# Attention and a routed feed-forward: another order of TensorE's work, other PSUM banks, and another way of filling the key windows

## The reference, cut to what matters

```
x: 2 x 2048 x 256 f32; 16 heads of 16; local causal attention, 64 back
qkv    = x @ W_attn + b_attn
scores = q k^T / 4, masked to j <= i and j >= i - 64;  attn = softmax(scores)
x = layernorm(x + (attn v) @ W_proj + b_proj)
e      = argmax(x @ Wr^T)                       # one of 8 experts for each token
inter  = gelu(x @ W1[e] + b1[e])                # 256 -> 1024
x = layernorm(x + layernorm(inter @ Wo + bo + x) * gamma + beta)
```

## Time and profile before

| what | us |
|---|---|
| median of three runs | 518.16 |
| the profiled execution: time | 519.47 |
| its span | 517.7 |
| PE busy | 486.7 (94%) |
| DVE busy | 406.8 (79%) |
| ACT busy | 356.0 (69%) |
| POOL busy | 277.0 (54%) |

### The profile page before, as it was taken

One profiled execution on the slowest core, in us unless ns is written; L12 is line 12 of the kernel. 1 busy time (PEld: TensorE's weight loads), 2 busy tenths in 40 slices (PEclk: granted clock), 3 DMA queues, 4 the chain that ended last, 5 costly groups with the idle time before them and its releaser, 6 DMA issues. The chain is left out here.

```text
span 517.7 us, 24448 instructions
## 1 busy us (share of the span) xinstructions
PE 486.7 (94%) x8597; PEld 431.7 (83%) x8597; DVE 406.8 (79%) x1096; ACT 356.0 (69%) x796; POOL 277.0 (54%) x483
## 2 busy tenths in 40 slices
PE   7999999999999999999988899999999999999970
PEld 6778888888887888888876788899999999999960
DVE  5658888778877897789789748988888877887771
ACT  6676868686867786777767566666666667666850
POOL 8712546454555455544543347666667566556553
PEclk9999999999999999999999899999999999999995
DMA  7785767786776696768662122222355555522100
GB/s 206 224 237 160 210 205 204 199 237 204 224 208 202 190 268 177 213 198 242 184 176 81 52 79 68 74 76 73 86 173 177 168 173 197 194 75 70 41 23 8
DMA packets 90183, 80.96 MB, mean 156 GB/s; under 512 B 36502, under 2 KB 83871, under 8 KB 90018
## 3 DMA queue, kind: packets, MB, share of 16 engines
q1 hardware_dynamic: 86720, 70.95, 47.6%
q0 software_dynamic: 3248, 8.41, 4.4%
q10 hardware_dynamic: 98, 0.04, 0.0%
HBM read 43.50 MB, written 23.55 MB: 130 GB/s over the span
## 5 line engine op out<-in xcount | busy, mean ns | idle before, releaser
L1423 PE MATMUL ps<-v_even,w_hi 128*128 128x128 f16 x1024 | 139.3, 219 | 0.5 <-issue 0.4
L1405 PE MATMUL ps<-wo_hi,ks 128*128 128x256 f16 (+1 forms) x576 | 128.5, 273 | 2.5 <-DVE ks L1099 2.5
L839 ACT ACTIVATE probs<-ps,b1T 128x128 f32<-128x128 f32 (+1 forms) x312 | 85.5, 360 | 59.5 <-PE ps L1423 37.5
L1423 PE MATMUL ps<-v_even,w_lo 128*128 128x128 f16 x512 | 107.9, 219 | 0.0
L1423 PEld LDWEIGHTS ps<-v_even,w_hi 128*128 x1024 | 96.4, 98 | 2.5 <-issue 1.0
L1166 DVE TENSOR_REDUCE mx<-ps 128x4 bf16<-128x512 f32 x128 | 82.9, 684 | 8.4 <-PE ps L1474 8.2
L1405 PE MATMUL ps<-wo_lo,ks 128*128 128x256 f16 (+1 forms) x288 | 78.5, 273 | 0.0
L1523 PE MATMUL ps<-v_even,probs 128*64 128x17 f32 x1024 | 70.2, 210 | 1.8 <-issue 1.8
L858 ACT ACTIVATE probs<-ps 128x512 f32<-128x512 f32 x128 | 69.6, 611 | 2.5 <-PE ps L1500 1.6
L1523 PE MATMUL ps<-v_odd,probs 128*64 128x17 f32 x1024 | 70.1, 210 | 0.6 <-issue 0.6
L1523 PEld LDWEIGHTS ps<-v_even,probs 128*64 128x64 f32 x1024 | 65.2, 138 | 5.7 <-issue 5.0
(11 more groups left out here) (245 smaller groups left out, 1237.7 us busy)
## 6 DMA issues: line engine op xcount, KB each, us to landing
qk_s<-qk_room SPq DMA_DIRECT2D x32, 256.0 KB, 2.8
w_in<-in_L_ffn_W_dram SPq DMA_DIRECT2D x16, 512.0 KB, 5.6
v_odd<-slots SPq DMA_DIRECT2D x64, 128.0 KB
qs<-qk_s SPq DMA_DIRECT2D x16, 384.0 KB
ks<-qk_s SPq DMA_DIRECT2D x16, 384.0 KB, 5.2
ks<-qk_s SPq DMA_DIRECT2D x32, 144.0 KB
v_even<-v_odd SPq DMA_DIRECT2D x63, 68.0 KB, 3.2
qk_s<-qk_room SPq DMA_DIRECT2D x32, 128.0 KB, 3.1
```

The lines of the kernel that those rows point to most:

```text
L839: last = nc.scalar.activation(g[1 - p][:, ic, n * w:(n + 1) * w], ps_h[1 - p][:, half, col + n * w:col + (n + 1) * w], ACT.Gelu, bias=b1T[ ...
L1405: ins = mm(ps_y[p][0:m], h[p][hs][:, ic, 0:m], wo[ws][:, ic, :], start=n == 0, stop=n == 3 * IC - 1)
L1423: up_ins = mm(ps_h[1 - p][:, half, col + m * w:col + (m + 1) * w], weights(ws, m, k, ic), sT[1 - p][ss][:, k, at], start=k + n == 0, stop= ...
```

## The change

PE's order in a turn becomes: projection, transposes of x, scores 0 and 1, values 0, scores 2 and 3, values 1, next values, transposes of the maxima (now a full 128 columns), queries and keys, transposes of the attention, transposed scores with the ranks between. The projection moves to bank 6, the transposes of x to bank 4, the ranks to bank 2 (the last of each stay in bank 1), so that several waits go and others come. DVE takes `y` and the logits first in its turn, ahead of the maxima; the splits of `w1` go in pairs into even turns, one ahead of DVE's copy of the transposed attention and one behind it. ACT copies the values of tile `it` at the head of turn `it`, behind the last exponentials of the tile before, where it copied those of `it + 1` in the middle of the turn before. SP stores each pair's queries and keys in two DMAs with nothing written twice, loads queries and block 1 in three DMAs each at the head of an even turn, and fills the window from block 1 by two SBUF to SBUF copies in the odd turn. The first pair keeps the old way.

```diff
-    qk_s = nc.dram_tensor("qk_s", [2, TILES // 2, P, 3, CC, 2 * P], f16, kind="Internal").ap()
+    qk_0 = nc.dram_tensor("qk_0", [2, P, 3, CC, 2 * P], f16, kind="Internal").ap()
+    qk_s = nc.dram_tensor("qk_s", [2, TILES // 2, P, 2, CC, 2 * P], f16, kind="Internal").ap()
...
-        mx = [sb(f"mx{k}", [P, P - ALIGNED], bf16) for k in range(2)]
+        mx = [sb(f"mx{k}", [P, P], bf16) for k in range(2)]
...
-            return ps[:, 0 if t >= LEAD else 4 + t % 2, 0:CC * P].rearrange("p (k t) -> p k t", k=CC)
+            return ps[:, 4 if t >= LEAD else 4 + t % 2, 0:CC * P].rearrange("p (k t) -> p k t", k=CC)
...
-        ps_proj = ps[:, 1, 0:C + E]
+        def ps_proj(t):
+            return ps[:, 6 if t < TILES - 1 else 1, 0:C + E]
...
+        def w1_lows(it):
+
+            lows_at = range(it - 2, it if it % 2 == 0 else it - 2) if it < TILES - 3 else w1_halves(it)
+            return [n for n in lows_at if a_tile(n)]
...
+            def stack(g, w, dst, landing):
+
+                for j in range(3):
+                    rows = dst[2 * j:ALIGNED:6]
+                    sp.dma_start(rows.rearrange("r (h m) n -> r h (m n)", m=CC),
+                                 qk_s[PARTS[w][j], g].rearrange("(h d) w m n -> w d h (m n)", d=HD)[w]).then_inc(landing, 16)
 
             def stacks_begin(g):
...
-                windows(g, 0, new, stack_ld[k])
+                stack(g, 0, qs[k], stack_ld[k])
+                if g > 1:
+                    sp.wait_ge(window_ld[1 - k], 16 * window_loads(g - 1))
+                stack(g, 1, ks[k][:, 1, :, :], second_ld[k])
 
             def stacks_end(g):
...
+                sp.wait_ge(second_ld[k], 16 * second_loads(g))
+                sp.dma_start(ks[k][0:ALIGNED:2, 0, :, BLK:2 * P], ks[k][0:ALIGNED:2, 1, :, 0:2 * P - BLK]).then_inc(window_ld[k], 16)
+                sp.wait_ge(second_ld[1 - k], 16 * second_loads(g - 1))
+                sp.dma_start(ks[k][0:ALIGNED:2, 0, :, 0:BLK], ks[1 - k][0:ALIGNED:2, 1, :, 2 * P - BLK:2 * P]).then_inc(window_ld[k], 16)
...
+                        if g > 0:
+                            sp.dma_start(qk_s[part, g].rearrange("p w m n -> p (w m n)"),
+                                         qk[g % 2][part].rearrange("p w m n -> p (w m n)")).then_inc(qk_st[g % 2], 16)
...
+                if a_tile(it - 1) and it < LAST - 2:
+                    exps(3, it - 1)
+                if a_tile(it) and it > 0:
+                    copy_v(it)
...
                 if cur:
+                    exps(0)
                     exps(1)
-                if cur:
                     exps(2)
-                    exps(3)
...
-                if it >= 0 and a_tile(it + 1):
-                    router_x(it + 1)
+                for n in w1_lows(it)[:1]:
+                    split_w1(n)
...
                     nc.vector.tensor_copy(attT[:, :, :, :], ps_attT).then_inc(attT_out, 1)
-                for n in w1_halves(it):
+                if it >= 0 and a_tile(it + 1):
+                    router_x(it + 1)
+                for n in w1_lows(it)[1:]:
                     split_w1(n)
...
                     if step == 0:
-                        pe.wait_ge(stack_ld[pair % 2], 16 * (pair // 2 + 1 + window_loads(pair)))
+                        wait(pe, place_done, (done - 1) // 2)
+                        pe.wait_ge(stack_ld[pair % 2], 16 * stack_loads(pair))
+                        if pair > 0:
+                            pe.wait_ge(window_ld[pair % 2], 16 * window_loads(pair))
...
-                scores(0)
+                    scores(0)
+                    scores(1)
                 if a_tile(old):
                     pe.wait_ge(attT_out, old + 1)
...
-                scores(1)
                 for t in turned(it):
                     pe.wait_ge(xin_ld[t % 3], 16 * (t // 3 + 1))
                     if t >= LEAD:
-                        pe.wait_ge(qkh_done, t)
-                        pe.wait_ge(qkl_done, t)
+                        wait(pe, exp_done, 4 * (it - 1) + 1)
...
+                if it != 0:
+                    scores(0)
+                    scores(1)
                 values(0)
```

More of the change, by code:

```diff
@@ L302, in attention_then_routed_ffn @@
         stack_ld = [sem(f"stack_ld{k}") for k in range(2)]
-        chunk_ld = [sem(f"chunk_ld{k}") for k in range(2)]
+        window_ld = [sem(f"window_ld{k}") for k in range(2)]
         second_ld = [sem(f"second_ld{k}") for k in range(2)]
@@ L368, in unit, with transfers, qk_stores, stack_loads @@
             return step % CC, step // CC, 2 * (step % CC) + step // CC
+        def transfers(g, at_first, later):
+            return sum(later if n else at_first for n in range(g % 2, g + 1, 2))
+        def qk_stores(g):
+            return transfers(g, 4, 2)
+        def stack_loads(g):
+            return transfers(g, 2, 3)
         def window_loads(g):
-            return sum(1 + (n > 0) for n in range(g % 2, g + 1, 2))
+            return transfers(g, 1, 2)
+        def second_loads(g):
+            return transfers(g, 1, 3)
         def turned(it):
@@ L849, in _, with exps @@
             for it in range(FIRST, LAST + 1):
-                def exps(step):
+                def exps(step, it=it):
                     u = unit(step)[2]
@@ L923, in _ @@
                     maxima_rows(1)
-                if cur:
-                    exps(0)
                 if it == FIRST:
@@ L933, in _ @@
                     act.wait_ge(qk_done, new + 1)
-                    wait(act, qk_st[new // 2 % 2], 16 * QK_STORES * (new // 4))
+                    wait(act, qk_st[new // 2 % 2], 16 * qk_stores(new // 2 - 2))
                     nc.scalar.activation(qk[new // 2 % 2][0][:, :, :, new % 2 * P:new % 2 * P + P].rearrange("p w m t -> p (w m) t"),
@@ L951, in _ @@
                         copy_rows(1, e, t)
+                    copy_v(0)
             walk_slots(body3)
@@ L1280, in _ @@
                     dve.wait_ge(rank_done, pair + 1)
-                    nc.vector.tensor_tensor(place[pair % 2][:, :, :], ps_rank,
+                    nc.vector.tensor_tensor(place[pair % 2][:, :, :], ps_rank(pair),
                                             place[1 - pair % 2][:, 2:3, :].broadcast_to([P, 3, E]), ALU.add)\
@@ L1294, in _ @@
                     dve.wait_ge(qkh_done, new + 1)
-                    wait(dve, qk_st[new // 2 % 2], 16 * QK_STORES * (new // 4))
+                    wait(dve, qk_st[new // 2 % 2], 16 * qk_stores(new // 2 - 2))
                     hi, lo = (qk[new // 2 % 2][s][:, :, :, new % 2 * P:new % 2 * P + P].rearrange("p w m t -> p (w m) t")
@@ L1441, in _ @@
             for it in range(FIRST, LAST + 1):
+                done, old, new = it - 1, it - 2, it + LEAD
                 def scores(step):
@@ L1502, in scores_t @@
                     last.then_inc(st_done, 1)
-                done, old, new = it - 1, it - 2, it + LEAD
                 def values(c):
@@ L1514, in values @@
                             pe.wait_ge(vlow_ld[done % 2], 16 * ((done + 1) // 2))
-                        wait(pe, att_done, done)
+                        wait(pe, lg_done, done)
                         if done == 0:
@@ L1546, in _ @@
                     warm(10)
-                scores(0)
+                    scores(0)
+                    scores(1)
                 if a_tile(old):
                     pe.wait_ge(attT_out, old + 1)
-                    wait(pe, v_out, upto(it))
-                    wait(pe, lx_done, upto(it))
-                    wait(pe, place_done, old // 2)
+                    if old == TILES - 1:
+                        pe.wait_ge(v_out, TILES)
+                        pe.wait_ge(place_done, old // 2)
                     if old == 0:
                         pe.wait_ge(wlo_done, 4)
-                    product(ps_proj, [(attT[:, 0, c, :], attT[:, 1, c, :]) for c in range(CC)],
+                    product(ps_proj(old), [(attT[:, 0, c, :], attT[:, 1, c, :]) for c in range(CC)],
                             [(wp[0][:, c, :], wp[1][:, c, :]) for c in range(CC)]).then_inc(proj_done, 1)
-                scores(1)
                 for t in turned(it):
```

113 lines of the change are left out of this document (57 added, 56 removed).

## The result

The changed kernel takes 525.31 us (median of 11 runs, 522.31 to 530.4), the kernel before 517.95 us (11 runs): a ratio of 1.0167, 95% interval 1.0134 to 1.0201. The forecast was 504.0, in 497 to 515. The profiled execution of the changed kernel took 522.69 us.

The account below looks back on a forecast made before the run. PE was taken to bound the attention loop at 8.46 us a turn. Borders 17.0 plus tail 0.8, less 1.5 for the DVE and POOL loop and 2.0 for windows, took 14.3 off 518.2: 504.0, range 497 to 515.

Parts of the forecast that it names:

- A clean turn of 7.53: An undisturbed attention turn on PE falls from 8.16 to 7.53 us, 17.0 us over 27 turns.
- Which borders cost: PE loses 0.09 to 0.125 us wherever the array columns in use change; borders removed sum to 0.63 a turn.
- Waits on the banks, 0: PE's new waits on exponentials, logits and places after the bank moves cost 0, bounds 0 and 0.1 us a turn.
- The loop through DVE and POOL, 1.5: Attention returns to PE with 0.3 us slack; a weight split beside POOL's second step adds 0.43 in even turns: 1.5 us.
- Windows, 2 charged: Window copies before scores 0 of even turns land in 5.2 us, within 5.1 to 5.4; 2 us charged for scatter.
- The 1 us to start in the forecast's sum: An estimated 1 us for the window copies to start, within the sums of 6.5 and 9.0 us for their landing.
- Tail, 0.8: Turns 28 to 31, without x and queries, gain 0.8 us for all four, between 0 and 2.5.
- The stalls at issue stay as they are: PE's stalls inside groups of matmuls, put down to issue, 0.30 us a turn, remain unchanged.
- the clock has nothing to give: TensorE's clock in the attention loop is 1.00, its 2.4 GHz level, so no gain can come from it.
- the prediction's two signs of being wrong: A clean turn above 7.8 us, or PE standing before scores 0 for over half a us in every pair.
- number 2: Windows land 5.6 to 6.3 us after issue, costing 0.3 to 1 us a pair: 509 to 516; chance 0.10.
- rival 3: Late windows replace the borders: gain gone at 6.5 us landing, 537 at 7.8; chance 0.08, at over 521.

Follow-up runs that it names:

- kernel 1: The changed kernel with the stores, stacks and windows of the kernel before given back, PE's order, banks and splits kept: 530.25 us, ratio 1.0266.
- kernel 3: The changed kernel with the w1 splits back to one a turn: 522.17 us, ratio 1.0068.
- kernel 4: The kernel before with only the maxima's transposes made 128 columns wide: 517.4 us, ratio 1.0018.
- kernel 5: The changed kernel with light transfers: stores, stacks, windows and w1 cut to an eighth, from the fourth pair and third w1 unit on: 506.74 us, ratio 0.9772.
- kernel 6: The kernel before with the same transfers cut to an eighth, from the fourth pair and third w1 unit on: 514.0 us, ratio 0.9931.
- kernel 7: The changed kernel with 128 more instructions, satisfied waits, ahead of TensorE's first warm-up: 543.64 us, ratio 1.0479.
- kernel 8: The kernel before with the same 128 instructions ahead of TensorE's first warm-up: 528.62 us, ratio 1.0223.
- kernel 13: The changed kernel with the whole w1 load moved in SP's list from ahead of the stores to behind them: 512.8 us, ratio 0.9873.
- kernel 17: The kernel before with the whole w1 load moved behind the stores: 513.41 us, ratio 0.9934.

## Why the prediction was wrong

- *A clean turn of 7.53*: right. 7.58 with the ranks, and 7.51 where there are neither ranks nor a w1 split beside POOL (kernels 1 and 3; in the changed kernel every other turn has the split and takes 7.75 or more).
- *Which borders cost*: right in nearly all, 0.60 a turn for 0.63 (the x and scores of turns with ranks gave less); in kernel 4 two of them gave 0.06 only, since another wait moved in.
- *Waits on the banks, 0*: wrong in small. Values wait 0.42 for the exponentials in turns 19 and 21 and 0.74 for the logits in turn 15, and shorter in four more: 3.4 us over the scores' clean time. In the light kernel, turns 15, 19, 21 and 24, it is 1.9.
- *The loop through DVE and POOL, 1.5*: right mechanism, price too low. Beside the split POOL's step takes 1.16 us for 0.67, and PE's queries 1.87 to 1.89 for 1.56, 0.31 in 13 turns: 4.0. The rows, POOL's first:

```profile
234.21 1.16 POOL L785 TENSOR_TENSOR att_lo<-att,att_hi 128x256 f16<-128x256 f32 x1
```

```profile
61.74 0.28 PE L1700 MATMUL ps<-ident_h,att_hi 128*128 128x128 f16 x2 [0.17 <-POOL att_lo L785]
```

- *Windows, 2 charged*: too low. 5.2 us of excess at the scores of turns 2, 10, 14, 18 and 28. The two copies land in 3.6 and 3.7 us in the median, faster than the 5.2 taken, but the pair issued at 99.59 took 6.0 with the w1 load at 102.21 behind it. The page DMA: Bandwidth & Descriptors of the Trainium skill (Why small descriptors are slow (HBM only)) spares SBUF to SBUF transfers the penalty of small pieces. The trace agrees in the median; the wait came from what stood before and beside them, and from the hop behind the stacks. The 1 us to start in the forecast's sum is a guess that no run here shows.
- *Tail, 0.8*: right; 1.1 with all that follows.
- **"The stalls at issue stay as they are"**, and with it that *the clock has nothing to give*: this step failed. I took a size that was measured at one speed of PE for a constant. The stalls on record in the kernel before, 2.5 us, were not even of the kind that then cost most: in the changed kernel 8.4 us stand at the packets' places, where the kernel before has 0.4, and the clock of 1.00 fell to 0.50 for 13.7 us, where the kernel before has none of it. With light transfers the changed kernel's turns are 6.2 us shorter than those of the kernel before (9.7 if the 3.5 of windows in its first turns, still of full size, are taken off); with full traffic they are 5.3 longer. The 11.5 between are 16.0 less 4.5. Neither of the prediction's two signs of being wrong came: a clean turn stayed below 7.8, and PE stood before the scores for over half a us in 4 of 14 pairs, not in every one. Both looked at the terms of the sum and none at what the sum held constant.
- The rivals: number 2 named windows at 509 to 516 and 3 at over 521; both had the place but not the cause, and neither their price. That 525.3 lies where rival 3 put it is luck: by rival 3 the windows land at 6.5 us and later in every pair, and they landed in 3.6 and 3.7 in the median, 6.1 at most. None had the transfers ahead of the windows, or PE's instructions.

The sum redone from the runs, on the turns: 27 x (8.16 - 7.53) = -17.0 forecast; a border sum of 0.60 for 0.63 +0.8, POOL +4.0, exponentials and logits +1.9; that makes -10.3 where light transfers give -9.7, and 0.6 is not explained. Then +3.5 for windows in the first pairs and +11.5 for traffic make +5.3.

Some of this stays open. That a late packet is what holds PE rests on the stalls' places in the stream, on kernels 5 to 8 and on the packets' times, not on a record of PE's fetch. Why the packets of the changed kernel begin later at worst (5.2 us after PE has passed the last place, 3.8 in the kernel before) was not tried, nor what decides whether a stall is followed by the slow clock. And kernels 13 and 17 stand at 512.8 and 513.4, measured at different times, with overlapping ratios, 0.9873 and 0.9934: once the order of transfers is mended, the regrouping itself is worth some 0.6%, and anything from nothing to 1.5% fits the intervals. With light transfers it is worth 1.4% (506.74 for 514.0).

The page Runtime: NRT & Kernel Launch of the Trainium skill (Instruction fetch mechanics) says of the border of a 16 KiB block that its cost is "one DMA tail-bump, mostly hidden". With light transfers the trace nearly agrees, 1.7 us in five stalls of kernel 5; with full ones it does not: 8.4 us in nine stalls of the changed kernel, and up to 3.04 us in one of kernel 1.

## What to carry to other kernels

- A stall on record is a price at the present speed. Before an engine's list is made shorter, look at what feeds it (instruction packets, loads a hop behind other loads) and work out whether that keeps the new pace.
- In a shared queue, put the transfer whose landing something waits for ahead of the large one that nobody needs soon. One moved DMA was worth 12.5 us here by the medians, 2.4% of the changed kernel, and 0.7% of the kernel before.
- Count hops: store, load, copy had to fit into two turns, and with faster turns they did not in some pairs.
- When "issue" ends an idle time, count where it stands in the engine's own stream. A fixed distance in instructions points at the fetch, a fixed place in the work at a wait.

## What the runs showed of the hardware

- The same list of TensorE instructions took 233.2 or 217.2 us for its turns depending on data traffic alone (share of the DMA engines 0.65 or about 0.34).
- PE's instructions move in packets of 16 KB, one for 257 records of its trace, and with full traffic PE could stand up to 3.04 us at such a place (kernel 1).
- 128 instructions on PE of two satisfied waits each, ahead of all work, took 13.2 us, 0.1 us an instruction.
- A wait could cost twice itself: PE's waits of 1.85 and 2.12 us were each followed by a turn that began at the 1.2 GHz level, at least 3.7 us of slower work for 3.97 of waits. No such turn followed those of 1.39 and 1.41. The length of a stall does not decide it: in kernel 4 the clock fell behind stalls of 0.80 and 0.82 us (turns 14 and 21), and in kernel 1 it stayed at 1.00 behind one of 3.04 (turn 3).
